# In the attention phase's step, the first quad's aggregates are issued ahead of the third quad's sums on TensorE

## The reference, cut to what matters

```
hi = x[src] @ w1 ; hj = x[tgt] @ w2
e  = leaky_relu(hi + hj, 0.3) * a
logits = e.reshape(-1, 8, 16).sum(-1)               # 8 heads
exp  = exp(logits - segment_max(logits, tgt)[tgt])
attn = exp / segment_sum(exp, tgt)[tgt]
out  = segment_sum(hi.reshape(-1, 8, 16) * attn[:, :, None], tgt)
x = layernorm(x + out)
```

## Time and profile before

| | |
|---|---|
| median of 2 runs | 2207.9 us (2207.4 and 2208.41) |
| the profiled execution | 2204.6 us, its span 2202.5 us |
| mean granted clock of TensorE | 0.899 of full |
| PE / PEld / DVE / ACT / POOL busy | 1800.7 / 1400.5 / 1327.6 / 658.6 / 1605.9 us |
| POOL's first and last gather of the first phase begin | 34.1 and 1089.3 us |
| POOL's first and last gather of the second phase begin | 1140.7 and 2182.0 us |

### The profile page before, as it was taken

The page is one execution under the profiler, slowest core; times in us unless marked ns, Lnnn a source line. Parts: engine busy times, 40 slices in busy tenths (PEclk is TensorE's granted clock), DMA queues, the critical chain, the costliest instruction groups (busy, mean ns, idle before and its releaser), DMA issues.

```text
span 2202.5 us, 47203 instructions
## 1 busy us (share of the span) xinstructions
PE 1800.7 (82%) x12728; PEld 1400.5 (64%) x12729; DVE 1327.6 (60%) x3726; ACT 658.6 (30%) x1410; POOL 1605.9 (73%) x1701
## 2 busy tenths in 40 slices
PE   6678777988788788788969878888888888888886
PEld 6456555666566566566757666666766676666665
DVE  6455665666656666566645456666566566665665
ACT  6111211211111111111114434444444344434442
POOL 5777777777777777777627777777777777777774
PEclk8798998889988998889889999999999999999897
DMA  8722332323323333233255444444444444444441
GB/s 220 159 85 78 89 96 83 96 85 96 95 84 95 96 88 96 85 96 97 60 142 154 138 126 141 127 140 129 141 126 140 129 141 127 132 137 139 129 126 42
DMA packets 239386, 252.31 MB, mean 115 GB/s; under 512 B 141011, under 2 KB 187720, under 8 KB 239315
## 3 DMA queue, kind: packets, MB, share of 16 engines
q1 hardware_dynamic: 185036, 141.15, 21.5%
q0 software_dynamic: 54000, 110.28, 18.0%
q10 hardware_dynamic: 288, 0.13, 0.0%
HBM read 233.20 MB, written 13.22 MB: 112 GB/s over the span
## 4 chain that ended last, share of the span: by engine, by line
POOL 48%; issue 21%; PE 14%; DVE 7%; DMA 4%; DVEq 2%; POOLq 1%; ACT 1%; SPq 0%; ACTq 0%
POOL T L742 27%; POOL G L708 20%; PE ps L1847 2%; PE ps L1824 2%; DMA G<-hi_rows,idx 2%; PE ps L1819 2%; PE ps L1851 1%; DMA T<-y_rows,idx 1%; PE ps L1780 1%; PE ps L2061 1%; PE ps L2052 1%; DVEq L1309 1%; DVE msg L1329 1%; PE ps L2067 1%; PE ps L2073 1%
## 5 line engine op out<-in xcount | busy, mean ns | idle before, releaser
L742 POOL DMA_INDIRECT T<-y_rows,idx x831 | 789.0, 950 | 303.7 <-issue 249.2
L708 POOL DMA_INDIRECT G<-hi_rows,idx x831 | 801.9, 965 | 267.8 <-issue 249.0
L2052 PE MATMUL ps<-G 128*128 128x64 f32 x1664 | 228.5, 284 | 126.8 <-DVE acc L1606 126.2
L2052 PEld LDWEIGHTS ps<-G 128*128 128x128 f32 x1664 | 217.0, 204 | 138.7 <-issue 137.4
L993 ACT ACTIVATE G<-G 128x512 f32<-128x512 f32 x208 | 131.1, 630 | 576.6 <-DVE G L1612 576.6
L1819 PE MATMUL ps<-ident,G 128*128 128x128 f32 x828 | 151.0, 312 | 174.9 <-issue 60.0
L2061 PE MATMUL ps<-wN,G 128*128 128x128 f32 x1664 | 255.7, 302 | 26.3 <-DVE T L1571 26.0
L1612 DVE TENSOR_TENSOR G<-ps,T 128x512 f32<-128x512 f32 x208 | 143.6, 691 | 217.0 <-DMA T<-y_rows,idx 202.3
L890 ACT ACTIVATE V<-ps 128x512 f32<-128x512 f32 x207 | 123.6, 597 | 474.3 <-PE ps L1824 472.3
L1300 DVE TENSOR_TENSOR V<-ps,V 128x512 f32<-128x512 f32 x207 | 141.9, 686 | 179.5 <-ACT V L890 175.5
L2073 PEld LDWEIGHTS ps<-msg,wE 128*128 128x128 f32 x832 | 168.5, 203 | 125.2 <-issue 111.0
(11 more groups left out here) (233 smaller groups left out, 2252.3 us busy)
## 6 DMA issues: line engine op xcount, KB each, us to landing
T<-in_edge_weight SPq DMA_DIRECT2D x103, 512.0 KB
Dbc<-block_destinations SPq DMA_DIRECT2D x69, 384.0 KB
T<-in_edge_attr SPq DMA_DIRECT2D x103, 256.0 KB
G<-hi_rows,idx POOLq DMA_INDIRECT x831
T<-y_rows,idx POOLq DMA_INDIRECT x831, 2.5
link<-scan_destinations SPq DMA_DIRECT2D x280, 16.1 KB
hi_rows<-T SPq DMA_DIRECT2D x12, 256.0 KB, 2.8
mX<-in_x SPq DMA_DIRECT2D x15, 192.0 KB
```

The lines of the kernel that those rows point to most:

```text
L708: pool.indirect_dma_start(out=G[:, s, t * C:(t + 1) * C], out_offset=None, in_=hi_d[:, :], in_offset=bass.IndirectOffsetOnAxis(ap=idx[:, s ...
L742: pool.indirect_dma_start(out=Yb[:, r, t * C:(t + 1) * C], out_offset=None, in_=y_d[:, :], in_offset=bass.IndirectOffsetOnAxis(ap=idx[:, r ...
L2052: ins = pe.matmul(aggP[:, 0:W], hS[i][:, n * C:(n + 1) * C], ohB[i][:, n * W:(n + 1) * W], start=(n == 0), stop=(n == 3))
```

## The change

On TensorE, in the step of the first phase, `aggregate(0)` and `sums(2)` change places. No instruction is added or taken away, no other engine's list changes, and the steps behind `run_steps` are as they were.

```diff
                     logits(f, s, 0)
+                    aggregate(0)
                     sums(2)
-                    aggregate(0)
                     if b is not None:
                         pe.wait_ge(s_r1, b + 1)
```

## The result

The changed kernel takes 2237.05 us (two runs, 2227.56 and 2246.53) against 2207.9: ratio 1.0138, interval 1.0106 to 1.0170. Four later runs of it gave 2246.4, ratio 1.0184 (1.0147 to 1.0221). I had forecast 2211 in a range up to 2232. The change is slower by something the runs can tell, though by less than 2%.

The account below looks back on a forecast made before the run. GpSimd's gathers were taken to bound the first phase: 2204.6 + 0 for the steps + 2 for gather length + 1 for the end = 2207.6; with the runs' median 3.3 higher, 2211 us, eight in ten 2198 to 2232.

Parts of the forecast that it names:

- The bound: First phase: GpSimd's gathers set the pace, 61.0 us for four steps, and TensorE follows.
- The moved wait: TensorE's step: standing 1.1 to 1.2 us for the message before aggregate(0), sums(2) 2.6 late, add(0) 1.7 late.
- The steps at the full clock: TensorE's steps under the change: 13.45 us for s = 3, 13.2 for s = 0, 13.7 for s = 1, 15.45 for s = 2.
- the round's sum: Four full-clock steps of the first phase: 55.8 us, 4.9 more than before, 5.2 below POOL's 61.0.
- the low clock has to fit into these 5.2: First phase: TensorE's 1.2 GHz time, about 4.5 us a round before and expected to fall, must stay within 5.2.
- the walk: Event-by-event reckoning of a changed full-clock step from the timeline of before; for s = 3, 13.45 us instead of 12.3.
- the rival's own "for it": Argument for the reserve being eaten: more short stands (1.2 us for the message, 0.5 for carry up) may lower the clock.
- 14 us of reserve: Slack between message and gather, some 14 us, that must be gone before POOL waits for messages.
- the reserve is eaten: Rival: TensorE and DVE's round passes 61.0, POOL waits for messages; 2228 or 2265, middle 2240; chance 0.10.
- The late end: End of first phase to first gather of y: 0.3 us later, up to 6 with a slow step's lag; +1 taken.
- The gathers' length: POOL's gathers lengthened by meeting VectorE's L1379: +2 us taken, anything from -11 to +24.
- rhythm rival: L1379 against POOL's gathers: meets them nearly every step, 2234 to 2250, chance 0.09; or never, 2195, chance 0.07.

Follow-up runs that it names:

- f2: Changed order, but the first quad's feature products read a constant tile, so aggregate(0) need not wait for the message, against the kernel before: ratio 1.0012.
- h3: First twelve steps in the changed order, the later ones in the order of before, against the kernel before: ratio 0.9995.
- h2: Changed kernel with VectorE's message ahead of the next one-hots, shortening TensorE's stand, against the kernel before: ratio 1.0022.
- i1: Changed kernel with two constant products that put nothing in the result issued ahead of aggregate(0), against the kernel before: ratio 1.0021.
- f0: The changed kernel again, no edit, on a chip like the first, against the kernel before: ratio 1.0184.
- f3: First twelve steps in the order of before, all later ones changed, against the kernel before: ratio 1.0133.
- f1: Order of before, but TensorE waits for the message ahead of the third quad's sums, against the kernel before: ratio 1.0191.
- h1: Changed kernel with five constant products issued ahead of aggregate(0), 2.4 us and too long a fill, against the kernel before: ratio 1.0300.

## Why the prediction was wrong

- **The bound** was read right: GpSimd's gathers paced the first phase, and in every version that keeps a reserve of a few us (before, f2, h3, h2, i1) the ratio is within 0.3% of 1.
- **The moved wait** was right, place and size: 1.18 us of standing against 1.1 to 1.2, L1900's wait 0.78 against 0.5, add(0) behind leaky(2).
- **The steps at the full clock** were put too short. The change's first trace has eight with s = 3, at 13.85 to 14.10 us (mean 13.97) against 13.45, and eight with s = 0, at 14.21 to 14.31 (mean 14.27) against 13.2. For s = 3 the base was at fault and not the 1.15 added: the step of rows 4 is one of the shortest, its next step begins 0.69 us behind L1373's end (1023.99 to 1024.68), while three other full-clock steps of before that waited for no rows (12.55 to 12.59 us) and all eight of the change have 1.19 to 1.25 there. The one in f0 that has 0.69 too takes 13.53. For s = 0 the delay was at fault as well: L1373 comes 1.6 us later than in the step behind rows 4 (12.96 against 11.36 us into the step), so the attention hid less of leaky(2)'s delay than I said. The other two kinds have no full-clock step there.
- **The step that failed** is the round's sum: "55.8 us for four steps, 4.9 more than before and still 5.2 below POOL's 61.0", and "the low clock has to fit into these 5.2". The round was 62.1 and 62.7. The two measured kinds alone add 1.6 us, which makes the full-clock round 57.4 if the walk of the other two holds, and leaves 3.6 us and not 5.2. The low clock then took up to 4.7 and 5.3 us, where I had 4.5 from before and expected fewer. Neither error alone is enough in the first trace: 55.8 + 4.7 is 60.5, and 57.4 with fewer than 3.6 stays below 61.0. By kinds, s = 2 took 17.84 instead of 15.45, s = 1 15.0 to 15.2 instead of 13.7, s = 0 14.8 to 15.2 instead of 13.2, s = 3 14.3 to 14.6. I had tied the low clock to single stands of 3 us and more, which did vanish (no stand over 2 us is left between 180 and 1080 us, against 17), but the time at 1.2 GHz did not: by the granted clock it is 13.7 us a round before, 13.5 and 17.3 in the change. I dismissed the short stands in the rival's own "for it".
- **The reserve.** "14 us of reserve" were counted as at hand. It is never made when the changed order runs from the start (0.8, 2.2, 3.0 us at the first three pairs of the first trace and never above 4.8; never above 6.0 in f0), and f3 shows that it would have been eaten anyway. The run thus paid both parts of the rival "the reserve is eaten", stalls and the late end. The rival's mechanism is the one that came; its point of decision (5.2 us of low-clock time) was named, its chance of 0.10 was far too low. Of its two times, 2228 is reckoned from 2211 and 2265 from 2208; from 2211 the second is 2268.
- **The late end** was put at 0.3 to 6 us with +1 taken; it cost 11.6, since TensorE was as late as the order let it be.
- **The gathers' length**: +2.9 us in the first trace, +2 forecast. That term and its bounds held, and neither rhythm rival came.

Shown by runs: the wait is the cause (f1, f2); the later steps' pace decides, not the start (f3, h3); the loss falls by more than the dose of the wait does (h2), and work put in the stand takes most of it back (i1). Not shown: how the loss divides between the longer chain and the clock. For the clock speaks i1, where work in the stand shortens the steps with s = 2 by 1.9 us. For the chain speak f1, with more clock granted than before and the same loss as the change, and h2, with less clock granted than the change and next to no loss.

## What to carry to other kernels

When two engines share a round close to the bound of a third, count the margin in the worst of their own states: here 5.2 us of margin in 61 was nothing, because 1.6 of it came from walking the shortest steps of their kind instead of the usual ones, and up to 4.7 went to the low clock, which short stands cost as well as long ones. Walk the usual step, and keep what low clock there was before until a trace shows it gone. Ask of every piece of work that is moved ahead whether its operands are there; a wait in an in-order queue delays all behind it, and the work moved ahead gained nothing (1017.97 by the walk against 1018.11). A reserve seen in a trace belongs to the order that made it, so don't spend it in the sum for another order.

## What the runs showed of the hardware that I had not expected

- TensorE's clock fell to 1.2 GHz behind two stands of 1.48 and 1.47 us with 1.1 us of work between them. In the first trace of the change it fell there in 13 of 13 steps (first stand 1.4 to 1.9 us, second 1.3 to 1.5), and in 0 of 13 with two constant products (1.13 us) in the second stand. The stands alone don't decide: a step of before with three of 1.19, 1.31 and 1.46 us (261 to 276 us) ran at the full clock to its end.
- An f32 product of 128x256 is two records, 0.24 us each at the full clock (ten records in 2.43 us in h1).
- The same program took 2206 us on two chips and 3250, 3343 and 3358 us on three others. On the first of these a gather took 0.949 us as elsewhere, and TensorE and VectorE stood up to 15.8 and 12.2 us where a register is loaded.
